# Softmax denominators of an attention stage: eight key tiles per sum, added by GpSimd pairs and two levels of accumulating DMAs

## The reference

```
c6 = silu(c) @ Wc + bc                       # six shifts, scales and gates
xm = ln(x) * (1 + sc_msa) + sh_msa
q, k, v = xm @ Wq + bq, xm @ Wk + bk, xm @ Wv + bv     # heads of 32; q = q / 32
w = softmax(einsum('bqhc,bkhc->bhqk', q, k), axis=-1)
x = x + g_msa * (einsum('bhqk,bkhc->bqhc', w, v) @ Wo + bo)
h = gelu((ln(x) * (1 + sc_mlp) + sh_mlp) @ W1 + b1)
x = x + g_mlp * (h @ W2 + b2)
```

## Time and profile before

| | us |
|---|---|
| median of 3 runs | 2892.97 (2891.18 to 2893.5) |
| the profiled execution, its time | 2893.33 |
| the profiled execution, its span | 2891.2 |
| TensorE busy | 2827.3 (98% of the span) |
| GpSimd busy | 2001.4 (69%) |
| VectorE busy | 1995.1 (69%) |
| ScalarE busy | 1375.4 (48%) |

### The profile page before, as it was taken

How to read it: one execution, slowest core, us unless ns; L and a number is a source line. 1 busy time by engine, 2 the same in 40 slices (tenths; PEclk the granted TensorE clock), 3 DMA queues, 4 the chain that set the end, 5 groups by cost and what they waited for, 6 DMA issues and landing times. The chain is left out here.

```text
span 2891.2 us, 40767 instructions
## 1 busy us (share of the span) xinstructions
PE 2827.3 (98%) x14713; PEld 1811.5 (63%) x14713; DVE 1995.1 (69%) x3320; ACT 1375.4 (48%) x2599; POOL 2001.4 (69%) x1015
## 2 busy tenths in 40 slices
PE   7999999999999999999999999999699999999998
PEld 5777755555555555555555555553488888888887
DVE  5556677777777777777777777773657656666754
ACT  2322266666666666666666666666311211221211
POOL 1000099999999999999999999997555555555453
PEclk9999999999999999999999999999799999999999
DMA  6555533414314314323323324302201101100000
GB/s 233 193 185 172 170 86 82 110 32 103 89 34 100 89 44 101 81 63 87 75 67 89 84 61 94 77 20 100 95 15 44 44 1 44 44 16 29 30 15 15
DMA packets 152767, 225.19 MB, mean 78 GB/s; under 512 B 31804, under 2 KB 48760, under 8 KB 152568
## 3 DMA queue, kind: packets, MB, share of 16 engines
q1 hardware_dynamic: 123036, 204.81, 25.9%
q10 hardware_dynamic: 29532, 17.79, 2.1%
HBM read 162.30 MB, written 58.97 MB: 77 GB/s over the span
## 5 line engine op out<-in xcount | busy, mean ns | idle before, releaser
L921 DVE TENSOR_REDUCE part_max<-m_bank 128x1 f32<-128x512 f32 x1972 | 1207.5, 681 | 385.2 <-PE m_bank L999 385.1
L902 ACT ACTIVATE probs<-s_bank 128x512 f32<-128x512 f32 x2048 | 1035.3, 626 | 196.4 <-PE s_bank L1016 192.3
L804 POOL TENSOR_TENSOR low_sum<-probs 128x1024 f32<-128x1024 f32 x248 | 588.4, 2382 | 80.4 <-ACT probs L902 80.3
L819 POOL TENSOR_TENSOR high_sum<-high_sum,probs 128x1024 f32<-128x1024 f32 x256 | 608.6, 2378 | 40.6 <-ACT probs L902 3.8
L1026 PE MATMUL y_bank<-probs,vs 128*32 128x512 f32 x4096 | 495.6, 602 | 0.0
L1395 ACT ACTIVATE h<-up_bank,vecs 128x512 f32<-128x512 f32 x128 | 88.0, 688 | 574.7 <-PE up_bank L1423 574.7
L1016 PE MATMUL s_bank<-qs,ks 97*128 97x512 f32 x768 | 317.9, 417 | 1.8 <-ACT probs L902 1.5
L1016 PE MATMUL s_bank<-late_parts,ks 97*128 97x512 f32 x768 | 319.0, 416 | 0.2 <-ACT probs L902 0.2
L812 POOL TENSOR_TENSOR high_sum<-probs 128x1024 f32<-128x1024 f32 x128 | 307.5, 2402 | 13.6 <-ACT probs L902 13.3
L1026 PEld LDWEIGHTS y_bank<-probs,vs 128*32 128x32 f32 x4096 | 107.3, 109 | 243.3 <-issue 134.3
L1016 PEld LDWEIGHTS s_bank<-qs,ks 97*128 97x128 f32 x768 | 144.4, 189 | 133.0 <-issue 78.0
(11 more groups left out here) (167 smaller groups left out, 4689.3 us busy)
## 6 DMA issues: line engine op xcount, KB each, us to landing
late_parts<-q_parts SPq DMA_DIRECT2D x96, 256.0 KB, 4.8
late_parts<-k_parts SPq DMA_DIRECT2D x72, 256.0 KB, 4.6
ks<-k_parts SPq DMA_DIRECT2D x72, 256.0 KB, 5.0
late_plain<-in_x SPq DMA_DIRECT2D x16, 1024.0 KB, 7.5
q_parts<-qk_out SPq DMA_DIRECT2D x32, 512.0 KB, 3.5
k_parts<-qk_out SPq DMA_DIRECT2D x32, 512.0 KB, 3.5
space_parts<-q_parts SPq DMA_DIRECT2D x48, 256.0 KB, 5.0
space_parts<-k_parts SPq DMA_DIRECT2D x48, 256.0 KB, 4.5
```

The lines of the kernel that those rows point to most:

```text
L804: pool.tensor_tensor(low_sum[:, (2 * c + half) % 4, :, :], probs[:, first % RING, hs, :], probs[:, (first + 1) % RING, hs, :], ALU.add).th ...
L819: pool.tensor_tensor(high_sum[:, c % 2, :, :], high_sum[:, c % 2, :, :], probs[:, (4 * c + r) % RING, hs, :], ALU.add).then_inc(high_step, 1)
L902: act.activation(probs[:, tile % RING, h, :], s_bank[(HPG * tile + h) % 3][:, :], ACT.Exp).then_inc(p_done, 1)
L921: v.tensor_reduce(part_max[:, i % 2, hs, c:c + 1], m_bank[ring.bank["max", i, n]][:, :], AX.X, ALU.max).then_inc(m_taken, 1)
```

## The change

- GpSimd adds only pairs, for all four heads, as two additions of 128 x 1024 each: `first_pair(c)` (tiles 0 and 1 of a quad) into `first_sum`, which has four places, and `second_pair(c)` (tiles 2 and 3) into `second_sum`, which has two (the second of them is the memory of `late.wo`).
- `fold_quad(c)`: a DMA that GpSimd issues with `accum_op` add puts the second pair onto the first, 128 rows of 2048 float32, 1 MB. `fold_half(h)`: the same from the quad 2h+1 onto the quad 2h. There are 124 and 62 of them.
- `sums(h)` multiplies the result of eight tiles by the ones, four products, at block 4h+7 (`due_sum`).
- `take_sum` comes once in eight tiles. The last iteration's quads are not folded: VectorE makes `last_first`, GpSimd `second_pair`, TensorE eight products for each.
- `y_buf` has two places, and the inverse, its way through DRAM, `normalise` and `store_y` come up to an iteration later. `Wo` is loaded near the end of the stage.

```diff
-def due_quad(b):
-    return (b - 3) // 2 if b >= 3 and b % 2 == 1 else None
+def due_sum(b):
+    if b >= N_BLOCKS - 3:
+        return LAST_HALF + b - (N_BLOCKS - 3)
+    return (b - 7) // 4 if b >= 7 and b % 4 == 3 else None
...
+        def first_home(c):
+            return first_sum[:, (0, 1, 2, 0)[c - LAST_QUAD] if c >= LAST_QUAD else c % 4, :, :]
...
-            sp.dma_start(late.wo[:, :, :], Wo.rearrange("(t p) n -> p t n", p=P)).then_inc(wo_in, 16)
             for i in range(N_IT - 1):
                 iteration(i)
+            sp.wait_ge(*quad_done(LAST_QUAD - 1))
+            sp.dma_start(late.wo[:, :, :], Wo.rearrange("(t p) n -> p t n", p=P)).then_inc(wo_in, 16)
...
+            def first_pair(c):
+                h = c // 2
+                if h >= 2 and c % 2 == 0:
+                    pool.wait_ge(d_done, h - 1)
+                if h >= 2 and c % 2 == 1:
+                    pool.wait_ge(half_folded, 16 * (h - 1))
+                for hs in PAIR:
+                    pool.wait_ge(p_done, HPG * (4 * c + 1) + hs.stop)
+                    pool.tensor_tensor(first_home(c)[:, hs, :], probs[:, 4 * c % RING, hs, :],
+                                       probs[:, (4 * c + 1) % RING, hs, :], ALU.add).then_inc(first_ready, 1)
+            def second_pair(c):
...
+                elif c >= 2:
+                    pool.wait_ge(*quad_done(c - 2))
+                for hs in PAIR:
+                    pool.wait_ge(p_done, HPG * (4 * c + 3) + hs.stop)
+                    pool.tensor_tensor(second_home(c)[:, hs, :], probs[:, (4 * c + 2) % RING, hs, :],
+                                       probs[:, (4 * c + 3) % RING, hs, :], ALU.add).then_inc(second_ready, 1)
+            def accumulate(onto, what):
+                return pool.dma_start(onto.rearrange("p h n -> p (h n)"), what.rearrange("p h n -> p (h n)"), accum_op=ALU.add)
+            def fold_quad(c):
+                pool.wait_ge(first_ready, 2 * c + 2)
+                pool.wait_ge(second_ready, 2 * c + 2)
+                accumulate(first_home(c), second_home(c)).then_inc(quad_folded[c % 2], 16)
+            def fold_half(h):
+                pool.wait_ge(*quad_done(2 * h))
+                pool.wait_ge(*quad_done(2 * h + 1))
+                accumulate(first_home(2 * h), first_home(2 * h + 1)).then_inc(half_folded, 16)
...
             for c in range(N_QUADS):
-                if c >= QPI and c % QPI == QPI - 1:
-                    normalise(c // QPI - 1)
+                if c % QPI == QPI - 2 and c // QPI >= 2:
+                    normalise(c // QPI - 2)
                 if c < LAST_QUAD:
-                    low(c, 0)
-                high_first(c)
-                high_more(c, 2)
-                high_more(c, 3)
+                    first_pair(c)
+                if c % 2 == 0 and 0 < c <= LAST_QUAD:
+                    fold_half(c // 2 - 1)
+                second_pair(c)
                 if c < LAST_QUAD:
-                    low(c, 1)
+                    fold_quad(c)
+            normalise(N_IT - 2)
...
             def slot_free(tile):
                 act.wait_ge(av_done, tile + 1)
+                if r == 0:
+                    act.wait_ge(*firsts(c))
+                if r == 2:
+                    act.wait_ge(second_ready, 2 * c + 2)
...
+            def sums(u):
...
+                if u < LAST_HALF:
+                    pe.wait_ge(half_folded, 16 * (u + 1))
+                    for h in range(HPG):
+                        last = add_up(u, h, first_home(2 * u)[:, h, :], True, True)
...
-    nc = bacc.Bacc("TRN2", target_bir_lowering=False, num_devices=1)
+    nc = bacc.Bacc("TRN2", target_bir_lowering=False, num_devices=1, dynamic_dma_scratch_size=1024)
```

More of the change, by code:

```diff
@@ L632, in __init__ @@
                 b, within = divmod(N_SC * i + s, 2 * HPG)
-                if within == 2 * HPG - 1 and due_quad(b) is not None and due_quad(b) <= LAST_QUAD:
-                    uses.append(("sum", due_quad(b)))
+                if within == 2 * HPG - 1 and due_sum(b) is not None and due_sum(b) <= LAST_HALF:
+                    uses.append(("sum", due_sum(b)))
         self.bank, self.count, self.free_after = {}, {}, {}
@@ L796, in _ @@
             pool.wait_ge(ones_row, BPB - 1)
[L798 to L805, removed]
@@ L841, in take_y, with take_sum @@
                 act.wait_ge(av_done, NKT * (i + 1))
[L842 to L850, removed]
+                if i >= 2:
+                    act.wait_ge(y_stored, 16 * (i - 1))
+                act.activation(y_buf[:, i % 2, :], y_bank[:, :], ACT.Copy).then_inc(y_taken, 1)
+            def take_sum(h):
+                act.wait_ge(d_done, h + 1)
+                if h >= HPI and h % HPI == 0:
+                    act.wait_ge(d_moved, 16 * h)
+                act.activation(d_raw[:, h % HPI, :], m_bank[ring.bank["sum", h]][:, :], ACT.Copy).then_inc(d_taken, 1)
             def take_last_sums():
-                act.wait_ge(d_done, N_QUADS)
-                act.wait_ge(d_moved, 16 * LAST_QUAD)
-                act.activation(d_raw[:, 0, :], m_bank[ring.bank["sum", LAST_QUAD]][:, :], ACT.Copy).then_inc(d_taken, 1)
+                act.wait_ge(d_done, LAST_HALF + QPI)
+                act.wait_ge(d_moved, 16 * LAST_HALF)
+                act.activation(d_raw[:, 0, :], m_bank[ring.bank["sum", LAST_HALF]][:, :], ACT.Copy).then_inc(d_taken, 1)
             def move_sums(i):
-                act.wait_ge(d_taken, QPI * (i + 1))
+                act.wait_ge(d_taken, HPI * (i + 1))
                 if i:
                     act.wait_ge(small_ready, i)
-                for q in range(QPI):
+                for q in range(HPI):
                     act.dma_start(d_small[:, q, :], d_raw[0:P:DH, q, :]).then_inc(d_moved, 16)
@@ L964, in _ @@
                     maximum(i + 1, n)
-                    if i and n == INVERT_AT:
-                        invert_small(i - 1)
                 negative(i + 1)
@@ L974, in _ @@
                         maximum(i + 2, n)
+                        if i and n == INVERT_AT:
+                            invert_small(i - 1)
+            invert_small(N_IT - 3)
             for q in range(QPI):
-                for half in range(2):
-                    last_low(LAST_QUAD + q, half)
-                if q == 1:
+                last_first(q)
+                if q == 2:
                     invert_small(N_IT - 2)
```

149 lines of the change are left out of this document (71 added, 78 removed).

## The result

The kernel after takes **2950.03 us** (median of four runs, 2949.34 to 2950.96), the kernel before 2892.19 in runs beside it: a ratio of 1.020, 95% interval 1.0182 to 1.0218. The forecast was 2841, so it missed by 109 us and on the other side. The profiled execution took 2950.25, with a span of 2948.4.

What follows compares the result with a forecast made beforehand. The prediction took TensorE to set the pace before the change and GpSimd after it, with a round of 25.3 us against 26.18: 2893.33 - 53 for the rounds + 1 for the stage's end = 2841 us, range 2784 to 2965.

Steps and rivals of the forecast that it cites:

- 15.1 + 3i + L: GpSimd's round of eight tiles in us, from its operations, three DMA issues and one 1 MB fold's landing; forecast 25.3.
- the 106 us of the 122 groups: TensorE's sums: 122 groups of four products go, at 0.87 us each, worth 106 us if TensorE sets the pace.
- i = 0.9: GpSimd's queue: the time one DMA issue takes, put at 0.9 us, with three issues in a round.
- the issue is dear: Rival on GpSimd's DMA issues: at 2.4 us each, 3118 us; decides from 1.2 us an issue; chance 0.08.
- Two passes for an add: DMA engines: an accumulating fold passes its data twice, since the old contents are read too; 5.9 us of data a megabyte.
- L = 7.5: Landing of a 1 MB fold, from the end of its issue to its semaphore: 7.5 us.
- a gap above 4 us: Sign in the profile: GpSimd's gap between `first_pair` and `second_pair` of even quads, forecast 2.8 us; above 4 means slower.
- Single late folds are absorbed and the averages decide: GpSimd against TensorE: about 6.6 us of give absorbs a single late fold, so only average rounds count.
- The ring: The slack between GpSimd's pair additions and the exponentials and blocks around them: about 6.6 us of give.
- the DMA engines are full: Rival: folds and loads need 25.7 us a round, -30 us if it holds; at 273 GB/s 3199 us; loss chance 0.05.
- The landing is the new wait: Rival: GpSimd stands in `fold_half` behind a fold taking over 8.4 us; 2939 us, or 3112 at worst; chance 0.20.
- If that cover failed: `y_buf`'s second place not hiding the later inverse: ScalarE stands still once an iteration, 32 x about 3 us at most.

Runs made afterwards that it cites:

- e3: The kernel after, with each fold shrunk to a sixteenth (512 bytes of each row instead of 8 KB), all issues and waits kept: 2782.27 us.
- e4: The kernel after with the folds dropped and their semaphores raised instead: 2784.03 us.
- e13: The kernel after with the second addition of `second_pair` made for one head instead of two from quad 2 on, all transfers kept: 2946.68 us.
- e10: The kernel after without any load of queries, keys and values behind the first, all folds kept: 2819.16 us.
- e2: The kernel after without the query loads from iteration 1 on: 2903.72 us.
- e7: The kernel after without `fold_half`: four tiles to a sum, 124 folds in place of 186, one more group of products in eight tiles: 2860.47 us.
- e8: The kernel after with folds that copy the second operand and do not add it, same bytes, places and waits: 2790.57 us.
- e11: e7 plus an additional accumulating 1 MB fold in every second quad, whose result nobody uses: 3002.27 us.
- e1: The kernel after with SyncE's query loads held back until a `fold_quad` has landed: 3012.55 us.
- e5: The kernel after with `fold_half` issued behind `second_pair` instead of ahead of it: 3018.20 us.
- e6: e5 with the sum that needs the folded half also moved one block later: 2982.78 us.
- e9: e6 with `normalise` one quad later as well and the store of `y_buf` two tiles later: 2940.47 us.

## Why the prediction was wrong

The step that failed is the one that makes the round out of GpSimd's queue alone, 15.1 + 3i + L with a constant L. The runs show in its place that a transfer lands later the more the DMA engines have to do: 23.8 us of demand in a round in which TensorE needs 24.4. In detail:

- **TensorE's part: right.** 560 rows as forecast, and for the 106 us of the 122 groups e3 and e4 show 108 to 110 without the folds' traffic. Undisturbed blocks take 5.79 and a round's floor is 24.4.
- **GpSimd's additions: right.** 4.69 us for a pair against 4.73, beside a DMA share of 0.88. They did not get longer.
- **The issue, i = 0.9: the term of the sum that was mis-sized.** Its own row shows 0.87, but the queue pays 1.53 from start to start when it had to wait, since 0.6 us of idle stand ahead of it. Three issues come to 1.9 us more than forecast, which is nearly the whole gap between a round of 25.3 and one of 27.05. But the sum does not show the cause. The 1.53 is above the 1.2 from which "the issue is dear" was to decide; e3 pays it for two issues in three and runs at TensorE's pace, and e13 took 2.1 us out of the same queue and gained 0.1. The rival's condition was met, its mechanism isn't what happened.
- **Two passes for an add: right in kind.** An add holds the engines 5.25 us and a copy 3.04, 1.73 times. The Trainium skill (Collectives: The Full Stack, "The bandwidth ceiling: the fold count and why AG ≠ RS ≠ AR") gives 1.93, measured between a collective that copies and one that adds: same direction, and the measured factor decides here. Its rate, by which the fold would have landed in 5.6 us, was too good: from the end of the issue the best took 6.0, the median 8.6.
- **L = 7.5, a constant: the assumption that failed.** The mean wait came out at 2.9 us (3.5 less the 0.6 that belong to the issue), where 2.8 was forecast. That agreement is luck. It is a mean of 0.8 and 5.1, and the landing is no property of the fold. From the start of the issue the median was 5.4 us for copies, 7.7 for adds without the loads (e10), 9.5 in the kernel after and 10.5 in e13, where GpSimd asked sooner. The sign that was to give the slower case away, a gap above 4 us, did not show in the mean (3.5). A round can't be put together from GpSimd's operations and a fixed L.
- **"Single late folds are absorbed and the averages decide": wrong.** The ring gives 6.6 us once. Every second round the wait takes 5.7, TensorE stood idle 41 times for over 0.4 us in the stage (103 us, the longest 7.3), where it never did before, and its clock fell to 1.2 GHz behind such gaps. A short round can't give back what a long one took, since TensorE needs 24.4 for it.
- **The rival "the DMA engines are full": undersized at 0.05.** Its demand was 25.7 us a round, more than the 23.8 measured, and its verdict was "-30 us if it holds". It took fullness for a threshold at 100%. The runs show a ramp: at 0.74 of the floor's round 23 us are lost, at 0.98 some 165. This is the mechanism that decided: e2, e7, e8, e10 lower the demand and gain 46 to 160 us, e11 puts it back and loses 142, e1, e5, e6, e9, e13 move or shorten something else and gain 10 us at most.
- **"The landing is the new wait", 2939 us: near in number, half right.** `fold_half` is where most of it shows, but e1 and e5 nearly remove that wait and are slower, so it is the place of the symptom.
- **The tail, the later inverse, `Wo`:** the 1 us of the tail is too small to be read, and the second place of `y_buf` covered the inverse (4.5 us of waits in all). "If that cover failed" was costed at 3 us an iteration on ScalarE; in e5 it is GpSimd that waits for the inverse, 139.6 us in 21 waits, 6.6 each.

How the lost time divides can be worked out from the traces. Between the first and the last `times_v`, TensorE is idle 111.6 us in the kernel after and 6.4 in e3, and it works 116.9 us at the lower clock against 3.4. Work takes twice as long there (3.64 us for 16 rows of `times_v` in place of 1.92), so half of 113.5 is an estimate of what the clock costs. That makes 105 us of idle time and 57 of slow work, 162 of the 167 us above the floor: a third of the price of late transfers is paid behind the gaps and not in them. Still open is how much of e11 is due to two folds issued back to back.

## What to carry to other kernels

Count the DMA engines as an engine with a busy time of its own: for each transfer its share of the sixteen, summed over a round and set against the round's floor. Here up to three quarters cost 8 to 36 us, 0.85 already 55 to 121, and close to 1 over 150. Price an accumulating DMA of this form at 1.7 copies. When work is moved onto the DMA engines, list all transfers with a deadline, the 8 KB ones too, whose landing time here grew most in proportion (1.4 to 7.0 us); and if taking one wait away makes another appear, look for the shared resource and stop moving waits: here giving back one fold in three (e7) turned 2.0% slower into 1.1% faster.

## What the runs showed of the hardware

- An 8 KB transfer that takes 1.4 us (`inv_rows`) or 2.1 (`neg_max_row`) takes 7.0 or 6.4 in the kernel with 1 MB folds (medians). In e10, where only the folds are left beside them, `neg_max_row` still takes 5.2, but `inv_rows` is back at 1.4. The Trainium skill (DMA: Bandwidth & Descriptors, "Queues, rings and completion order") says that each engine goes round its queues a whole packet at a time, and not byte by byte; the rows of `neg_max_row` agree in kind, and no run here tells the size of the packets.
- A DMA issue behind a wait costs GpSimd's queue 1.53 us with an add and about 1.2 for a copy (median of e8's `fold_quad`, start to start less a pair), though the rows of the issues themselves read 0.87 and 0.57. The issue's row starts 0.60 us behind the landing that it waited for (1314.21 to 1314.81). Where it has nothing to wait for, it costs 0.6 (e3).
- GB/s misleads beside accumulates: 187 GB/s fill 0.88 of the engines here, while 350 fill 0.98 in the earlier trace rows.
